# Mixtures of experts: one buffer for each gathered and each result tile, all gathers asked for before the first scatter, and transposes and up products run further ahead

## What is computed

```python
# blocks 4 and 6 (kind 1): one expert of 8 for each token
expert_idx = jnp.argmax(x @ router_w + router_b, axis=-1)
for e in range(8):
    sel = x + 0.1 * game_emb[e]
    h = jax.nn.gelu(jnp.einsum('bsh,hi->bsi', sel, w1[e]) + b1[e], approximate=False)
    y = jnp.einsum('bsi,ih->bsh', h, w2[e]) + b2[e]
    out = jnp.where((expert_idx == e)[..., None], y, out)
# blocks 7 and 9 (kind 2): the best two of 8 experts for each token
topv, topi = jax.lax.top_k(jax.nn.softmax(xf @ router_w.T), 2)
topv = topv / (topv.sum(axis=-1, keepdims=True) + 1e-09)
h = jax.nn.gelu(jnp.einsum('td,edh->teh', xf, w1), approximate=False)
y = jnp.einsum('teh,ehd->ted', h, w2)          # weighted by topv and summed over e
```

## Time and profile before

| what | value |
|---|---|
| median of 3 runs | 1891.1 us (1890.85 to 1893.7) |
| profiled execution: its span, from the first to the last instruction | 1895.7 us |
| busy: PE / DVE / ACT / POOL | 80% / 56% / 50% / 19% |
| mean granted clock of TensorE | 0.893 of full |
| loop of mixture 1 (23 tiles): first gather to start of last scatter | 193.11 to 268.25 us |
| loop of mixture 2 (23 tiles) | 658.56 to 732.37 us |
| loop of mixture 3 (39 tiles) | 766.71 to 887.01 us |
| loop of mixture 4 (39 tiles) | 1355.70 to 1477.04 us |

### The profile page before, as it was taken

One profiled execution on the slowest core, in us unless ns is written; L12 is line 12 of the kernel. 1 busy time (PEld: TensorE's weight loads), 2 busy tenths in 40 slices (PEclk: granted clock), 3 DMA queues, 4 the chain that ended last, 5 costly groups with the idle time before them and its releaser, 6 DMA issues. The chain is left out here.

```text
span 1895.7 us, 27344 instructions
## 1 busy us (share of the span) xinstructions
PE 1516.1 (80%) x9044; PEld 827.3 (44%) x9102; DVE 1055.2 (56%) x2297; ACT 939.8 (50%) x2171; POOL 367.1 (19%) x512
## 2 busy tenths in 40 slices
PE   4895757999999586775599898987577885988879
PEld 4454653555555375665222222222477552222245
DVE  6576331333334524312788988894611575788656
ACT  3454334444444334112387787875311434777733
POOL 1230530000000163564030101000266101101000
PEclk7796877999999788798699999998688896999989
DMA  2002434120200343544320303000444304223000
GB/s 71 5 1 86 142 92 122 26 67 1 67 1 1 110 141 111 188 128 120 86 79 1 78 1 96 1 1 1 140 131 120 98 6 113 64 60 79 1 1 22
DMA packets 96180, 126.09 MB, mean 67 GB/s; under 512 B 14336, under 2 KB 65408, under 8 KB 95664
## 3 DMA queue, kind: packets, MB, share of 16 engines
q1 hardware_dynamic: 86384, 105.23, 19.3%
q0 software_dynamic: 7936, 16.27, 3.2%
q10 hardware_dynamic: 1728, 2.88, 0.7%
HBM read 87.54 MB, written 36.80 MB: 66 GB/s over the span
## 5 line engine op out<-in xcount | busy, mean ns | idle before, releaser
L2119 DVE TENSOR_REDUCE MAXI<-psum 128x2 f32<-128x1024 f32 x384 | 457.2, 1220 | 90.4 <-PE psum L1926 88.6
L2036 ACT ACTIVATE EX<-psum 128x512 f32<-128x512 f32 x768 | 412.8, 606 | 107.0 <-PE psum L1947 106.9
L1947 PE MATMUL psum<-QM,KM 64*128 64x512 bf16 x768 | 227.4, 383 | 32.3 <-ACT EX L2036 21.4
L2420 PE MATMUL psum<-EX,N 128*128 128x512 f32 x512 | 238.0, 608 | 0.0
L2482 ACT ACTIVATE EX<-psum 128x512 f32<-128x512 f32 x256 | 149.2, 598 | 173.7 <-PE psum L2412 173.7
L1926 PE MATMUL psum<-KM,QS 64*128 64x512 bf16 x768 | 184.5, 401 | 35.3 <-DVE MAXI L2119 14.9
L1957 PE MATMUL psum<-EX,VST 128*32 128x512 f32 x1536 | 203.1, 604 | 1.0 <-ACT OT L2050 1.0
L1382 DVE TENSOR_SCALAR m_Y<-psum 128x128 f32<-128x128 f32 x124 | 36.0, 290 | 280.6 <-PE psum L1165 159.9
L1165 PE MATMUL psum<-m_DOWN,m_H 128*128 x992 | 148.6, 298 | 48.0 <-issue 30.9
L1151 PE MATMUL psum<-m_XT,m_W 128*128 128x128 f32 x992 | 154.4, 306 | 18.8 <-DVE m_XT L1375 13.7
L1165 PEld LDWEIGHTS psum<-m_DOWN,m_H 128*128 128x128 f32 x992 | 135.6, 212 | 53.5 <-issue 53.2
(11 more groups left out here) (330 smaller groups left out, 2020.7 us busy)
## 6 DMA issues: line engine op xcount, KB each, us to landing
m_W<-in_w_dram SPq DMA_DIRECT2D x124, 256.0 KB
parts<-PART SPq DMA_DIRECT2D x24, 384.0 KB, 2.6
m_DOWN<-in_w_dram SPq DMA_DIRECT2D x32, 256.0 KB, 4.8
parts<-PART SPq DMA_DIRECT2D x24, 256.0 KB, 2.4
rows<-N SPq DMA_DIRECT2D x16, 256.0 KB, 3.1
N<-y SPq DMA_DIRECT2D x16, 256.0 KB, 4.0
QS<-parts SPq DMA_DIRECT2D x32, 128.0 KB, 3.7
QS<-parts SPq DMA_DIRECT2D x16, 256.0 KB, 5.9
```

The source lines that it names most:

```text
L1947: pe.matmul(bank_of(("score", n, i)), KM[r, buf, g, m, kt * P:(kt + 1) * P], QM[r, n % 2, MAPS[at] // slots, :], start=True, stop=True).th ...
L2036: act.activation(EX[:, n % 2, kt, MAPS[j], :], bank_of(("score", n, i)), ACT.Exp, scale=SM_SCALE).then_inc(S["exp"].sem, 1)
L2119: dve.tensor_reduce(MAXI[:, n % 2, qt, columns], pair(i), AX, ALU.max, negate=True).then_inc(S["reduced"].sem, 1)
L2420: last = pe.matmul(banks[4 + j], N[:, n // per_b * TB + kt, :], EX[:, n % 2, kt, j, :], start=kt == 0, stop=kt == TB - 1)
```

## The change

Only the loop of `moe` is changed. Every tile gets its own buffer in `XG` and in `Y`. GpSimd asks for all R gathers first and then for all R scatters. At most 6 gathers and 4 scatters are in flight: gather r waits until gather r - 6 has landed, and scatter r waits for y(r) and until scatter r - 4 has landed. TensorE transposes 5 tiles ahead (`TURNS`) and runs the up product 2 tiles ahead in kind 1 and 3 in kind 2 (`UPS`); `XT` has 6 buffers, `H` has `UPS` + 1, and the up product has 3 or 4 PSUM banks instead of 2. The four bias products of kind 1 share one bank and stand two iterations apart. y(r) no longer waits for a scatter.

```diff
-        AHEAD, DEEP = 8, 5
+        DEEP = 5
+        TURNS, UPS = 5, 2 if one else 3
+        XS, HS = 6, UPS + 1
+        IN_FLIGHT, OUT_FLIGHT = 6, 4
...
-        XG = sb("XG", [P, AHEAD, P])
-        XT = sb("XT", [P, 2, P])
-        H = sb("H", [P, 2, IT * P])
-        Y = sb("Y", [P, 3, P])
+        XG = sb("XG", [P, R, P])
+        XT = sb("XT", [P, XS, P])
+        H = sb("H", [P, HS, IT * P])
+        Y = sb("Y", [P, R, P])
...
+        up_banks = [banks[i] for i in (2, 3, 4, 7)[:UPS + 1]]
+
+        def turn_at(r):
+            return banks[r % 2][:, 0:P]
+
+        def down_at(r):
+            return banks[5 + r % 2][:, 0:P]
 
...
                 def gather(r):
-                    if r >= AHEAD:
-                        pool.wait_ge(S["turned"].sem, S["turned"].at(r - AHEAD + 1))
-                    pool.indirect_dma_start(XG[:, r % AHEAD, :], None, rows_dram,
+                    if r >= IN_FLIGHT:
+                        pool.wait_ge(gathered[r % IN_FLIGHT].sem, gathered[r % IN_FLIGHT].at(16 * (r // IN_FLIGHT)))
+                    pool.indirect_dma_start(XG[:, r, :], None, rows_dram,
                                             bass.IndirectOffsetOnAxis(ap=ROWS[:, 0, r:r + 1].bitcast(U32), axis=0)
-                                            ).then_inc(gathered[r % AHEAD].sem, 16)
+                                            ).then_inc(gathered[r % IN_FLIGHT].sem, 16)
 
                 def scatter(r):
                     pool.wait_ge(S["y"].sem, S["y"].at(r + 1))
+                    if r >= OUT_FLIGHT:
+                        pool.wait_ge(scattered[r % OUT_FLIGHT].sem, scattered[r % OUT_FLIGHT].at(16 * (r // OUT_FLIGHT)))
                     pool.indirect_dma_start(y_dram, bass.IndirectOffsetOnAxis(ap=ROWS[:, 1, r:r + 1].bitcast(U32), axis=0),
-                                            Y[:, r % 3, :], None).then_inc(scattered[r % 3].sem, 16)
+                                            Y[:, r, :], None).then_inc(scattered[r % OUT_FLIGHT].sem, 16)
 
                 if fix_now:
                     self.fill_fixed(pool, FIX)
                 pool.wait_ge(stored.sem, stored.at(16 * (B + 1)))
                 pool.wait_ge(S["indexed"].sem, S["indexed"].at(1))
-                for r in range(AHEAD):
+                for r in range(R):
                     gather(r)
                 for r in range(R):
                     scatter(r)
-                    if r + AHEAD < R:
-                        gather(r + AHEAD)
 
             @block.tensor
             def _(pe):
...
                 def turn(r):
-                    pe.wait_ge(gathered[r % AHEAD].sem, gathered[r % AHEAD].at(16 * (r // AHEAD + 1)))
+                    pe.wait_ge(gathered[r % IN_FLIGHT].sem, gathered[r % IN_FLIGHT].at(16 * (r // IN_FLIGHT + 1)))
                     if r >= 2:
                         pe.wait_ge(S["xt"].sem, S["xt"].at(r - 1))
-                    pe.transpose(banks[r % 2][:, 0:P], XG[:, r % AHEAD, :], self.ident[:]).then_inc(S["turned"].sem, 1)
+                    pe.transpose(turn_at(r), XG[:, r, :], self.ident[:]).then_inc(S["turned"].sem, 1)
 
                 def up(r):
                     pe.wait_ge(S["xt"].sem, S["xt"].at(r + 1))
                     pe.wait_ge(weights[r % DEEP].sem, weights[r % DEEP].at(16 * (r // DEEP + 1)))
-                    if r >= 2:
-                        pe.wait_ge(S["gelu"].sem, S["gelu"].at(r - 1))
+                    if r > UPS:
+                        pe.wait_ge(S["gelu"].sem, S["gelu"].at(r - UPS))
                     for it in range(IT):
-                        last = pe.matmul(banks[2 + r % 2][:, it * P:(it + 1) * P], W[:, r % DEEP, it * P:(it + 1) * P],
-                                         XT[:, r % 2, :], start=True, stop=True)
+                        last = pe.matmul(up_banks[r % len(up_banks)][:, it * P:(it + 1) * P], W[:, r % DEEP, it * P:(it + 1) * P],
+                                         XT[:, r % XS, :], start=True, stop=True)
                     last.then_inc(S["up"].sem, 1)
 
                 def expert(r):
@@ -1162,16 +1172,16 @@
                     if r >= 2:
...
                 turn(0)
                 turn(1)
                 up(0)
+                turn(2)
+                turn(3)
+                up(1)
+                turn(4)
+                for r in range(2, UPS):
+                    up(r)
                 for r in range(R):
-                    if r + 2 < R:
-                        turn(r + 2)
-                    if r + 1 < R:
-                        up(r + 1)
+                    if r + TURNS < R:
+                        turn(r + TURNS)
+                    if r + UPS < R:
+                        up(r + UPS)
                     down(r, of)
                     if r + 1 < R:
                         of = expert(r + 1)
-                    if one and r in (2, 3, 6, 7):
-                        bias((2, 3, 6, 7).index(r))
+                    if one and r in (2, 4, 6, 8):
+                        bias((2, 4, 6, 8).index(r))
                 if self.routes:
...
                     act.wait_ge(S["up"].sem, S["up"].at(r + 1))
-                    if r >= 2:
-                        act.wait_ge(S["down"].sem, S["down"].at(r - 1))
+                    if r >= HS:
+                        act.wait_ge(S["down"].sem, S["down"].at(r - HS + 1))
...
                 def y(r):
                     dve.wait_ge(S["down"].sem, S["down"].at(r + 1))
-                    if r >= 3:
-                        dve.wait_ge(scattered[r % 3].sem, scattered[r % 3].at(16 * (r // 3)))
-                    dve.tensor_scalar(Y[:, r % 3, :], banks[4 + r % 2][:, 0:P], 0.5 if one else 1.0, None, ALU.mult
+                    dve.tensor_scalar(Y[:, r, :], down_at(r), 0.5 if one else 1.0, None, ALU.mult
                                       ).then_inc(S["y"].sem, 1)
...
-                xt(0)
-                xt(1)
+                for r in range(TURNS):
+                    xt(r)
                 for r in range(R):
-                    if r + 2 < R:
-                        xt(r + 2)
+                    if r + TURNS < R:
+                        xt(r + TURNS)
```

More of the change, by code:

```diff
@@ L1062, in moe @@
         resident = self.semaphore_of("moe_resident")
-        gathered = [self.semaphore_of(f"moe_gathered{i}") for i in range(AHEAD)]
-        scattered = [self.semaphore_of(f"moe_scattered{i}") for i in range(3)]
+        gathered = [self.semaphore_of(f"moe_gathered{i}") for i in range(IN_FLIGHT)]
+        scattered = [self.semaphore_of(f"moe_scattered{i}") for i in range(OUT_FLIGHT)]
         weights = [self.semaphore_of(f"moe_weights{i}") for i in range(DEEP)]
@@ L1096, in _ @@
                                  ).then_inc(weights[r % DEEP].sem, 16)
-                for i in range(3):
-                    sp.wait_ge(scattered[i].sem, scattered[i].at(16 * len(range(i, R, 3))))
+                for i in range(OUT_FLIGHT):
+                    sp.wait_ge(scattered[i].sem, scattered[i].at(16 * len(range(i, R, OUT_FLIGHT))))
                 for b in range(B):
@@ L1164, in down @@
                     for it in range(IT):
[L1165 removed]
+                        last = pe.matmul(down_at(r), H[:, r % HS, it * P:(it + 1) * P], DOWN[:, bass.ds(e, 1), it * P:(it + 1) * P].rearrange("p e n -> p (e n)"),
                                          start=(it == 0), stop=(it == IT - 1))
@@ L1210, in _ @@
                         of = expert(r + 1)
-                    if one and r in (2, 3, 6, 7):
-                        bias((2, 3, 6, 7).index(r))
+                    if one and r in (2, 4, 6, 8):
+                        bias((2, 4, 6, 8).index(r))
                 if self.routes:
                     unread(3, 12)
-                    for i in range(3):
-                        pe.wait_ge(scattered[i].sem, scattered[i].at(16 * len(range(i, R, 3))))
+                    for i in range(OUT_FLIGHT):
+                        pe.wait_ge(scattered[i].sem, scattered[i].at(16 * len(range(i, R, OUT_FLIGHT))))
                     unread(3, 10)
@@ L1243, in _ @@
                             s = slice(it * P, (it + 1) * P)
-                            last = act.activation(H[:, r % 2, s], banks[2 + r % 2][:, s], ACT.Gelu, bias=B1[:, r, it:it + 1])
+                            last = act.activation(H[:, r % HS, s], up_banks[r % len(up_banks)][:, s], ACT.Gelu, bias=B1[:, r, it:it + 1])
                     else:
-                        last = act.activation(H[:, r % 2, :], banks[2 + r % 2], ACT.Gelu)
+                        last = act.activation(H[:, r % HS, :], up_banks[r % len(up_banks)], ACT.Gelu)
                     last.then_inc(S["gelu"].sem, 1)
@@ L1437, in moe @@
         resident.passed(16 * E)
-        for i in range(AHEAD):
-            gathered[i].passed(16 * len(range(i, R, AHEAD)))
-        for i in range(3):
-            scattered[i].passed(16 * len(range(i, R, 3)))
+        for i in range(IN_FLIGHT):
+            gathered[i].passed(16 * len(range(i, R, IN_FLIGHT)))
```

(2 more changed lines are left out.)

23 lines of the change are left out of this document (11 added, 12 removed).

## The result

| | median | runs | span of the profiled execution | clock |
|---|---|---|---|---|
| before | 1890.97 us | 1890.84 to 1893.7 (4) | 1895.7 us | 0.893 |
| after | 1912.48 us | 1908.72 to 1913.88 (4) | 1911.3 us | 0.877 |

The ratio is 1.0115 (95% interval 1.010 to 1.0129): 1.2% slower, where 3.8% faster was forecast.

What follows compares the result with a forecast made beforehand. It took the loops to be bound by a chain of waits between engines with only 2 or 3 buffers. Terms -77.3 + 5 + 1 = -71 us gave a span of 1824.7, a median 4.6 below, 1820 us; range 1803 to 1848.

Steps and rivals of the forecast that it cites:

- What bounds the kernel now: Loops: neither TensorE (1.90 us a tile) nor GpSimd (2.57) is full; a chain of waits with few buffers gives 3.08.
- GpSimd's term: Four loops: GpSimd issues gathers 1.26 us apart, then scatters 1.29 apart, waiting for no one; -77.3 us together.
- New waits on landings: Loops: gather r waits for gather r - 6, scatter r for scatter r - 4, both landed in time; cost 0.
- second waits: From each loop's fifth scatter on, 108 scatters have two waits; bounds 0 to 65 us, taken as 0.
- Rival C: Loops: the second wait is paid in full on 108 scatters, 65 us lost, 1885 us; chance 0.08.
- E: Loops: burst gathers take 1.88 us each, not 1.26, as DMA engines can't serve them; no change; chance 0.05.
- TensorE's term: Loops: TensorE keeps ahead of GpSimd at 1.90 us a tile; late signals add 2.5 us per kind 1 loop, 5 in all.
- The evidence I used against lateness: Loop 1's start: eight gathers issued without a pause in 10 us, transposes following at once; held against late signals.
- Rival D: Handover from up product to gelu, kind 1: lateness grows with unbroken DMA issue; at 6 us a tile, 1920 us; chance 0.06.
- The prediction's last sentence: Loops: the forecast would be most wrong if late signals are caused by GpSimd's DMAs and grow with them; no size.

Runs made afterwards that it cites:

- chip A: Chip of the first set of follow-up runs; there the kernel before the change takes 1826.9 us.
- paced one: Changed kernel with a 0.54 us memset on GpSimd behind each gather: 1869.9 us (1.0234 of the kernel before), and on another chip 1895.2 us (1.0018).
- B, C and D: Chips of the later follow-up sets; there the kernel before the change takes 1895.3, 1890.6 and 1890 us.

## Why the prediction was wrong

- **What bounds the kernel now: the rows were right, the reading was not.** I took the 1.9 us for which GpSimd waits in a cycle for slack that deeper buffers release (0.30 of it is the usual gap between two DMAs; beyond three times 2.57, a cycle of 9.23 leaves 1.5). By the experiments the wait was itself made by GpSimd's DMAs: their pace holds up the results that GpSimd then waits for. Read so, the 3.08 us a tile were two indirect DMAs of 1.54, not 2.57 and a chain of waits. On chip A the kernel before would run at GpSimd's pace: a span near 1825 less 1506 outside leaves some 319 us for 124 tiles, 2.57 each. That is argued from its times; no profile of it there was taken.
- **GpSimd's term (-77.3 us): its pace for gathers right, for scatters not reached.** 1.25 us against 1.26 for gathers. Scatters stood 1.89 apart, not 1.29, since the results came late.
- **New waits on landings (0) and second waits (0): right.** Gathers issue with 0.30 us between them throughout, and scatters behind two waits with 0.30 as well (nearly all on chip A, the last three of loop 3 on the first chip). Rival C is out. So is E: 1.25 us, not 1.88.
- **TensorE's term (+5 us): this is the step that failed.** It held that TensorE keeps up with GpSimd at 1.90 us a tile, with 2.5 us added for each loop of kind 1 and "nothing to add" in kind 2. The loops came out 13.1 us longer instead of 77.3 shorter, so what came on top of GpSimd's term is 13.1 + 77.3 = 90.4 us, not 5. Worst was kind 2, where I had 14 us of spare. Loop 3 is 47.6 us of gathers in which no tile's result was copied, 7.9 us until the first scatter, and 69.2 us from first to last scatter (900.23 - 831.06) at TensorE's pace.
- **The evidence I used against lateness misled.** The eight gathers at a loop's start have their transposes at once, and I concluded that a burst does no harm. The lateness piles up. In loop 3 of the changed kernel a transpose's signal is still prompt at 784.49, when the eighth gather is issued; the first late one is that of the up product over at 786.16, behind the ninth. The first gelu starts at 783.08, the second ten and the third thirty microseconds later. Eight gathers were too few to show it.
- **Rival D (0.06) had the sign and nearly the mechanism**: lateness grown with the unbroken issue. It was sized from the largest row shown, 3.3 us (loop 3 of the kernel before has them up to 4.9), put to 6 us on every tile of kind 1 alone. It was up to 41 us on a handful of TensorE's signals, to VectorE and ScalarE alike and in kind 2 as much. The prediction's last sentence named the cause, and the sum ignored it.
- **Open.** What it is that an indirect DMA occupies, whether the step or the number in flight sets it, whether the recording takes part, and why chip A shows none of it. The changed kernel did not run on chip A. From the paced one an estimate can be made: loops of 363.7 us less 0.41 for each of 120 gathers is 314.5, with 1504 outside 1818 us of span, so about 1820 against 1826.9. Even there most of the forecast gain would be missing, because the kernel before seems to have no lateness to lose.

## What to carry to other kernels

A wait with a releaser that the trace can't name, on several engines at once, is a cause to find before any buffer is added: here it went with the pace of the very DMAs that the change made denser. On the chips that show it, indirect DMAs 1.66 us or more apart on average left the other engines alone; yet none of the paced kernels beat the one before by more than 0.2%: 78 DMAs 1.66 us apart are 129 us, more than the 120 of its loop 3. So fewer of them, or plain ones where the rows lie in order, is what is left to try. An interleaved queue can be a brake that a burst removes, and a short burst that does no harm is no evidence for a long one.

## What the runs showed of the hardware

- On the first chip and on B, C and D, indirect gathers at a mean step of 1.45 us or less, and scatters at 1.27, made TensorE's semaphores rise up to 43 us late for ScalarE and VectorE, and TensorE's own products start 2.10 us apart; at 1.66 us or more, and with plain DMAs seven in 3.82 us, signals were at most 1.1 us late.
- The same kernel takes 1826.9 us on one chip and 1890 to 1895 on others. On the one, none of four kernels shows a late signal; on the others, all do. The kernel before was not profiled on it. The paced kernel is 2.3% slower than before on chip A and 0.2% on chip C: a version's worth depends on the chip it is measured on.
